# Cross-attention and a table-GELU feed-forward on one core: bias work, clears and one product moved, and TensorE products that nobody reads in the opening

## The chip, the core and the metric

The kernel runs on one core of a Trainium2 chip. The metric is the device time of one launch in microseconds (us), the median of several runs. The engines are named as the profile names them: PE is TensorE (matmuls and transposes), DVE is VectorE, ACT is ScalarE, POOL is GpSimd, SP is the engine that issues most DMAs.

## The reference, cut to what matters

Tokens: 64 sequences of 64, each of width 128, so 4,096 rows. The context has the same shape.

```
q  = layernorm(x) @ Wq.T + bq           # 16 heads of 8
kv = ctx @ Wkv.T + bkv                  # k and v interleaved in the last axis
q, k = rms_norm(q) * q_gamma, rms_norm(k) * k_gamma
x  = x + softmax(q k^T / sqrt(8)) v     # within each sequence of 64

h  = layernorm(x) @ w1 + b1             # 128 -> 512
h  = round(h * 256) / 256
h  = interp(h, 33 points of GELU on [-4, 4]), 0 below, identity above, rounded again
x  = x + round((h @ w2 + b2) * 256) / 256
```

## The kernel before

Each engine has its own instruction stream, written out by hand, and they meet only at semaphores. An engine runs its stream strictly in the order in which it is written. There is no scheduler.

**Setup.** The two projection weights are loaded and transposed on PE, and DVE copies them out of PSUM (L698 to L704). Biases are added by a matmul: a bias row is split into three float16 parts that sum to it (`bias_parts`, stages 0 to 4, L719 to L727) and multiplied by a matrix that picks the parts. This is done once for the attention (`B_Q` to `B_1`) and once for the feed-forward (`ffn_bias`), where `w1` and `b1` are also scaled by 256 (L790, L794). Four buffers `v_blk` hold v in blocks, zero elsewhere, with ones that give the softmax's denominator. They are cleared once, 0 and 1 by DVE (`clear_v`, L590), 2 and 3 by POOL (L382), and POOL writes the ones (L371, L387).

**Attention.** There are 16 steps of 2 tiles (256 tokens). `step(s)` on each engine does the stages of several neighbouring steps, as a software pipeline, and starts with `step(-3)`, `step(-2)` or `step(-1)`. For step s + 1 DVE's `step(s)` does `mean_square` (L617, needs ACT's square L435), `bias_v` (L654, needs PE's `project_v` L974), `normalise` (L624) and `highs` (L635, L637), for step s `copy_parts` (L644), for s - 1 `heads_out` (L664, L666), for s - 2 the feed-forward's layer norm (`ln2_statistics` L606, `norm_x2` L611), and for s + 3 `ln_statistics` (L600). POOL's `step(s)` does `norm_x` for s + 2 (L309 to L315), `lows` for s + 1 (L334), and smaller pieces. PE's `step(s)` does `transpose_parts(s)` (L992), `times_v(s - 1)` (L1022), `project_v(s + 1)`, `scores(s)` (L1006), `transpose_in(s + 2)` (L943, L948), `out_back(s - 1)` (L1032) and `project_qk(s + 2)` (L955, L935, L960, L964). `transpose_in(s)` waits for `bias_v(s - 1)`, and `project_qk(s)` for `normalise(s - 1)`, since they share PSUM banks.

**Feed-forward.** There are 8 groups of 4 tiles, each in two units of 1,024 columns. Per unit: hidden product (PE, L1128 and L1129), rounding (ACT, L513), split into segment and fraction (DVE, `f_segment` L829, `f_fraction` L835), two GELU look-ups (ACT, L521 and L530), difference and slope (DVE, `f_rise` L842, `f_slope` L850), the sum (POOL, `f_interpolate` L406, which waits for a `frac_ready` of the next group), rounding (DVE, `f_round` L856), down product (PE, L1144), and the residual (DVE, `f_out` L862). Between the two parts PE writes the first hidden product in two halves (`hidden_first(0)` and `(1)`, L1163), which DVE rounds (`round_first`, L818).

**Start of the attention.** DVE's stream goes `step(-2)`, then `scale_w1` and the first half of the feed-forward's bias work, then `step(-1)`, then the rest of it, then `step(0)`. POOL's stream goes `step(-2)`, ones for two buffers, `step(-1)`, clears and ones for the other two, `step(0)`. A check of a bound on the scores (`guarded`) stands between. It loads one value and branches, and its body isn't run with these inputs.

Of the kernel before, what the change touches and what calls it, by code (L numbers as in the profile page):

```python
# [40 lines left out]
P = 128  # L41
# [31 lines left out]
def xattn_ffn(nc, x_d, ctx_d, wq_d, bq_d, wkv_d, bkv_d, gq_d, gk_d, w1_d, b1_d, w2_d, b2_d, out_d):  # L73
# [11 lines left out]
    with ctx:  # L85
# [210 lines left out]
        def _(pool):  # L296
# [69 lines left out]
            pool.wait_ge(S["v_zeroed"], 2)  # L366
            for k in range(2):
                for half in range(2):

                    wait(pool, "blocks_set", 2 * k + half)  # L370
                    g.memset(v_blk[k][64 * half:64 * half + 64, :, :, half, DH:DH + 1].rearrange("p b q e -> p b (q e)"), 1.0).then_inc(S["blocks_set"], 1)  # L371
            pool.wait_ge(S["blocks_set"], 4)
# [8 lines left out]
            for k in range(2, 4):  # L381
                g.memset(v_blk[k][:, :, :, :, :].rearrange("p b q h e -> p (b q h e)"), 0.0).then_inc(S["v_zeroed"], 1)  # L382
            pool.wait_ge(S["v_zeroed"], 4)
            for k in range(2, 4):
                for half in range(2):
                    wait(pool, "blocks_set", 2 * k + half)
                    g.memset(v_blk[k][64 * half:64 * half + 64, :, :, half, DH:DH + 1].rearrange("p b q e -> p b (q e)"), 1.0).then_inc(S["blocks_set"], 1)  # L387
            pool.wait_ge(S["blocks_set"], 8)
# [192 lines left out]
        def _(dve):  # L581
# [146 lines left out]

            dve.wait_ge(S["small_loaded"], 16 * 4)
# [62 lines left out]
            ffn_bias = slice(B_1, B_END)  # L792
            scale_w1()
# [3 lines left out]
            step(-1, 3)  # L797
            for stage in range(2, 5):
                bias_parts(ffn_bias, stage, "ffn_ready")
            for s in range(0, LOOP_FROM):  # L800
                step(s, s % 4)
# [62 lines left out]
            def group(gr):  # L864
                f_rise(gr, 0)
                f_slope(gr, 0)
                if gr >= 1:
                    f_round(gr - 1, 1)
                if gr + 1 < GROUPS:
                    f_segment(gr + 1, 0)  # L870
                    f_fraction(gr + 1, 0)
                if gr == 1:
                    norm_x2(STEPS - 1)
# [23 lines left out]
            ln2_statistics(STEPS - 2)  # L897
            f_segment(0, 1)
            f_fraction(0, 1)
            norm_x2(STEPS - 2)  # L900
# [23 lines left out]
        def _(pe):  # L924
            t_ = nc.tensor
            pe.wait_ge(S["wqkv_loaded"], 16 * 2)
            pe.wait_ge(S["identity_ready"], 1)
# [3 lines left out]
            last.then_inc(S["w_transposed"], 1)  # L931

# [241 lines left out]
            scores(last_step, 0)  # L1174
            scores(last_step, 1)
# [3 lines left out]
            hidden_first(0)  # L1179
            out_back(last_step - 1)  # L1180
# [61 lines left out]
```

## Time and profile before

| | |
|---|---|
| median of 3 runs | 220.64 us (218.24 to 221.98) |
| the profiled execution | 219.01 us, of which the trace's span is 217.1 us |
| PE busy | 184.1 us (85%) |
| DVE busy | 189.3 us (87%) |
| ACT busy | 146.3 us (67%) |
| POOL busy | 117.9 us (54%) |
| mean granted TensorE clock | 0.959 |

In the trace the opening takes 0 to 32 us, the steady attention steps 32 to 118 us, the turn to the feed-forward 118 to 140 us and the feed-forward the rest. A row of a timeline gives the start, the duration of the group, engine, line, operation, operands, the count, and in brackets how long the engine was idle before it and what ended that.

### The profile page before, as it was taken

Reading aid. Unit: us, or ns where it says so; the run is one execution under the profiler, and the core shown is the slowest. Engines: PE = TensorE matmul, PEld = TensorE weight load, DVE = VectorE, ACT = ScalarE, POOL = GpSimd, SP = SyncE. Lnnn points to the kernel's source line nnn. Section 1 sums busy time; section 2 is a strip of 40 time slices with the busy share of each in tenths; the row PEclk is TensorE's granted clock in tenths of the full one; section 3 lists DMA queues with packets and bytes.
Section 4 is the critical chain, followed back from the end, with each engine's and each line's share of the span. In section 5 each row is a group of like instructions: output and inputs, shape, how many; then the busy total and the mean of one; then the engine's idle time right before and its main releaser. Section 6 shows DMA issues by size and latency. Waiting matters only on the chain.

```text
span 217.1 us, 8020 instructions
## 1 busy us (share of the span) xinstructions
PE 184.1 (85%) x3308; PEld 143.5 (66%) x3308; DVE 189.3 (87%) x348; ACT 146.3 (67%) x226; POOL 117.9 (54%) x166
## 2 busy tenths in 40 slices
PE   1172889999999999999999789959799999986693
PEld 0161768888888888888888645456566566654592
DVE  6628968799999999999999757999999999999992
ACT  2021367778977778987777778867487878878511
POOL 7330864687677687767675501465165444655430
PEclk9996699999999999999999999988999999999679
DMA  4270111011211011100000000000101011010103
GB/s 110 82 206 10 51 53 49 14 44 51 54 53 49 27 32 53 51 27 29 8 3 3 3 3 2 3 0 0 48 5 48 0 48 51 0 48 0 48 0 97
DMA packets 14835, 7.95 MB, mean 37 GB/s; under 512 B 1072, under 2 KB 14576, under 8 KB 14800
## 3 DMA queue, kind: packets, MB, share of 16 engines
q1 hardware_dynamic: 14272, 7.20, 11.6%
q8 instruction: 26, 0.43, 0.8%
q10 hardware_dynamic: 528, 0.25, 0.4%
q14 instruction: 9, 0.07, 0.1%
HBM read 5.35 MB, written 2.10 MB: 34 GB/s over the span
## 4 chain that ended last, share of the span: by engine, by line
PE 44%; DVE 23%; issue 13%; POOL 13%; DMA 2%; ACT 1%; SPq 1%; DVEq 0%; POOLq 0%; ACTq 0%
POOL y_raw L406 8%; PE bank_o L1022 8%; PE banks_p L992 7%; PE banks_p L964 5%; PE banks_s L1006 5%; DVE frac L835 4%; DVE banks_p L842 4%; PE banks_p L974 4%; PE bank_o L1032 4%; PE banks_p L960 3%; DMA bkv_rep<-in_L_xattn_bkv_dram 2%; DVE y_raw L850 2%; DVE act_q L856 2%; PE banks_p L943 2%; DVE seg L829 2%
## 5 line engine op out<-in xcount | busy, mean ns | idle before, releaser
L406 POOL TENSOR_TENSOR y_raw<-g_lo,y_raw 128x1024 f32<-128x1024 f32 x15 | 35.4, 2363 | 36.4 <-DVE frac L835 35.4
L1144 PEld LDWEIGHTS bank_o<-w,act_q 128*128 128x128 f32 x224 | 29.9, 211 | 6.6 <-DVE act_q L856 5.9
L460 ACT ACTIVATE probs<-banks_s 128x512 f32<-128x512 f32 x64 | 33.0, 610 | 1.2 <-PE banks_s L1006 1.1
L334 POOL TENSOR_TENSOR parts<-qk_hat,parts 128x512 f16<-128x512 f32 x16 | 18.6, 1160 | 26.6 <-DVE parts L635 26.6
L1144 PE MATMUL bank_o<-w,act_q 128*128 128x128 f32 x224 | 31.4, 299 | 1.5 <-DVE act_q L856 1.3
L1129 PE MATMUL banks_s<-x2T,w 128*128 128x512 f32 x60 | 31.2, 602 | 0.0
L521 ACT ACTIVATE g_lo<-seg,gelu_lo 128x1024 f32<-128x1024 f32 x16 | 18.4, 1150 | 9.1 <-DVE seg L829 9.1
L530 ACT ACTIVATE banks_p<-seg,gelu_hi 128x1024 f32<-128x1024 f32 x16 | 17.9, 1118 | 8.8 <-DVE y_raw L850 8.8
L992 PE MATMUL banks_p<-ident,parts 128*128 128x128 f16 x256 | 19.6, 219 | 1.8 <-POOL parts L334 1.6
L1022 PE MATMUL bank_o<-probs,v_blk 128*32 128x64 f32 x1024 | 20.7, 222 | 0.0
L611 DVE TENSOR_SCALAR xn_all<-x_all,stats,rstd 128x128 f32<-128x128 f32 x32 | 20.1, 667 | 0.0
L850 DVE SCALAR_TENSOR_TENSOR y_raw<-banks_p,frac 128x1024 f32<-128x1024 f32 x16 | 19.6, 1224 | 0.5
L842 DVE TENSOR_TENSOR banks_p<-banks_p,g_lo 128x1024 f32<-128x1024 f32 x16 | 19.6, 1224 | 0.4 <-ACT banks_p L530 0.4
L430 ACT ACTIVATE xcT<-banks_p 128x512 f32<-128x512 f32 x16 | 9.6, 597 | 13.7 <-PE banks_p L948 13.7
L1022 PEld LDWEIGHTS bank_o<-probs,v_blk 128*32 128x32 f32 x1024 | 15.7, 109 | 3.9 <-issue 0.9
L992 PEld LDWEIGHTS banks_p<-ident,parts 128*128 128x128 f16 x256 | 14.8, 97 | 4.8 <-issue 2.0
L455 ACT ACTIVATE outT<-bank_o 128x512 f32<-128x512 f32 x16 | 9.5, 597 | 12.3 <-PE bank_o L1022 12.3
L450 ACT ACTIVATE partsT<-banks_p 128x1024 f16<-128x1024 f16 x16 | 16.4, 1022 | 0.8 <-PE banks_p L992 0.8
L513 ACT ACTIVATE hz<-banks_s,round_c 128x1024 f32<-128x1024 f32 x15 | 16.4, 1096 | 0.0
L1129 PEld LDWEIGHTS banks_s<-x2T,w 128*128 128x128 f32 x60 | 11.7, 195 | 6.8 <-issue 5.7
L943 PE MATMUL banks_p<-ident,c_in 128*128 128x128 f32 x32 | 7.4, 316 | 9.6 <-DVE wqgT L749 4.9
L654 DVE TENSOR_TENSOR v_blk<-banks_p,bv_rep 64x256 f32<-64x256 f32 x32 | 13.5, 421 | 2.1 <-PE banks_p L974 0.7
(114 smaller groups left out, 427.4 us busy)
## 6 DMA issues: line engine op xcount, KB each, us to landing
x_all<-in_x_dram SPq DMA_DIRECT2D x16, 128.0 KB, 2.9
c_in<-in_ctx_dram SPq DMA_DIRECT2D x16, 128.0 KB, 2.4
out_dram<-x_all SPq DMA_DIRECT2D x7, 256.0 KB, 2.3
w<-in_L_ffn_w_dram SPq DMA_DIRECT2D x2, 256.0 KB, 3.2
out_dram<-x_all SPq DMA_DIRECT2D x2, 128.0 KB, 1.9
b_rows<-in_L_ffn_b_dram SPq DMA_DIRECT2D x1, 192.0 KB, 3.6
wkv_raw<-in_L_xattn_Wkv_dram ACTq DMA_DIRECT2D x1, 128.0 KB, 2.9
bkv_rep<-in_L_xattn_bkv_dram SPq DMA_DIRECT2D x1, 128.0 KB, 5.4
```

The lines of the kernel that those rows point to most:

```text
L334: g.tensor_tensor(low_slot, qk_hat[:].rearrange("p w t (h d) -> p w (t h) d", d=DH), high_slots[:, :, :, 0, :], ALU.subtract).then_inc(S[" ...
L406: g.tensor_tensor(y_raw[u][:], g_lo[n % 3][:], y_raw[u][:], ALU.add).then_inc(S[f"gelu{u}_done"], 1)
L460: a.activation(probs[i][:].rearrange("p t g n -> p (t g n)"), bank_s(i), ACT.Exp).then_inc(S["probs_ready"], 1)
L521: a.activation(g_lo[n % 3][:], seg0[u][:], ACT.Gelu, bias=gelu_lo[:], scale=1.0 / FIX).then_inc(S["glo_ready"], 1)
L530: a.activation(g_hi, seg0[u][:], ACT.Gelu, bias=gelu_hi[:], scale=1.0 / FIX).then_inc(S["ghi_ready"], 1)
L611: v.tensor_scalar(xn2_all[:, tok(s, t, 2)], x_all[:, tok(s, t, 2)], stats2[:, t, 1:2], rstd2[:, t:t + 1], ALU.subtract, ALU.mult).then_inc ...
L842: v.tensor_tensor(g_hi, g_hi, g_lo[n % 3][:], ALU.subtract).then_inc(S["rise_ready"], 1)
L850: v.scalar_tensor_tensor(y_raw[u][:], g_hi, 1.0 / SEG, frac[u][:], ALU.mult, ALU.mult).then_inc(S["slope_done"], 1)
L992: last = t_.transpose(bank_qkT[:, c0:c0 + P], rows[:, P * k:P * k + P], ident16[:])
L1022: last = t_.matmul(bank_o[ROWS * i:ROWS * i + ROWS, c0:c0 + 64], v_blk[par][:, 2 * t + b, 2 * i + gg, :, :].rearrange("p h e -> p (h e)"), ...
L1129: last = t_.matmul(out, w1[:, f0:f0 + P], x2T[gr % 2][:], start=False, stop=True)
L1144: last = t_.matmul(out, act_q[u][:, c, P * t:P * t + P], w2[:, CH // UNITS * u + c, :], start=False, stop=(u == UNITS - 1 and t == GT - 1 ...
```

## The change

- PE: at its start 6, and after the weights' transposes 10, matmuls of the 128x128 identity with 512 columns of it, float16, into `bank_o`, which nobody reads there (`keep_busy`).
- DVE: `clear_v(2)` is added behind the copies of the weights. `step(-1)` now stands ahead of `scale_w1` and the first half of the feed-forward's bias work, `step(0)` ahead of stages 2 and 3, `step(1)` ahead of stage 4.
- POOL: the clear of `v_blk` 3 and all the ones go between `step(-2)` and the bound check. `v_blk` 2 is no longer POOL's.
- PE at the turn: `hidden_first(0)` and its waits go ahead of the last step's `scores`.
- DVE in the feed-forward: `norm_x2(STEPS - 2)` goes ahead of `f_segment(0, 1)`, and in group 1 `norm_x2(STEPS - 1)` ahead of `f_segment(2, 0)` and `f_fraction(2, 0)`.

```diff
@@ gpsimd
             step(-2)
-            pool.wait_ge(S["v_zeroed"], 2)
-            for k in range(2):
+            g.memset(v_blk[3][:, :, :, :, :].rearrange("p b q h e -> p (b q h e)"), 0.0).then_inc(S["v_zeroed"], 1)
+            pool.wait_ge(S["v_zeroed"], 4)
+            for k in range(4):
                 for half in range(2):
                     wait(pool, "blocks_set", 2 * k + half)
...
-            pool.wait_ge(S["blocks_set"], 4)
+            pool.wait_ge(S["blocks_set"], 8)
...
             step(-1)
-            for k in range(2, 4):
-                g.memset(v_blk[k][:, :, :, :, :].rearrange("p b q h e -> p (b q h e)"), 0.0).then_inc(S["v_zeroed"], 1)
-            pool.wait_ge(S["v_zeroed"], 4)
-            for k in range(2, 4):
-                for half in range(2):
...
@@ vector
+            clear_v(2)
             dve.wait_ge(S["small_loaded"], 16 * 4)
...
+            step(-1, 3)
             scale_w1()
             setup(v.tensor_scalar(b_rows[:, B_1:B_2], b_rows[:, B_1:B_2], FIX, None, ALU.mult))
             bias_parts(ffn_bias, 0, "ffn_ready")
             bias_parts(ffn_bias, 1, "ffn_ready")
-            step(-1, 3)
-            for stage in range(2, 5):
-                bias_parts(ffn_bias, stage, "ffn_ready")
-            for s in range(0, LOOP_FROM):
+            step(0, 0)
+            bias_parts(ffn_bias, 2, "ffn_ready")
+            bias_parts(ffn_bias, 3, "ffn_ready")
+            step(1, 1)
+            bias_parts(ffn_bias, 4, "ffn_ready")
+            for s in range(2, LOOP_FROM):
                 step(s, s % 4)
...
+                if gr == 1:
+                    norm_x2(STEPS - 1)
                 if gr + 1 < GROUPS:
                     f_segment(gr + 1, 0)
                     f_fraction(gr + 1, 0)
-                if gr == 1:
-                    norm_x2(STEPS - 1)
...
             ln2_statistics(STEPS - 2)
+            norm_x2(STEPS - 2)
             f_segment(0, 1)
             f_fraction(0, 1)
-            norm_x2(STEPS - 2)
@@ tensor
+            def keep_busy(n):
+                for _ in range(n):
+                    t_.matmul(bank_o[:], ident16[:], ident16[:].unsqueeze(1).to_broadcast([P, 4, P]), start=True, stop=True)
+
+            pe.wait_ge(S["identity_ready"], 1)
+            pe.wait_ge(S["consts_ready"], 1)
+            keep_busy(6)
             pe.wait_ge(S["wqkv_loaded"], 16 * 2)
-            pe.wait_ge(S["identity_ready"], 1)
...
             last.then_inc(S["w_transposed"], 1)
+            keep_busy(10)
...
-            scores(last_step, 0)
-            scores(last_step, 1)
             pe.wait_ge(S["ffn_ready"], 2)
             pe.wait_ge(S["qk_normed"], STEPS)
             pe.wait_ge(S["x2_t_copied"], 2)
             hidden_first(0)
+            scores(last_step, 0)
+            scores(last_step, 1)
             out_back(last_step - 1)
```

DVE around `step(-1)`, before. The first four rows are the scaling and stages 0 and 1, the six from `ms` to `stats` are `step(-1)`, and the two behind them are stages 2 and 3 (`b_rest` holds what is left of a bias after its float16 part):

```order
L790 TENSOR_SCALAR w1<-w1 128x512
L794 TENSOR_SCALAR b_rows<-b_rows 96x512
L719 CAST b_parts<-b_rows 96x640
L721 TENSOR_TENSOR b_rest<-b_rows,b_parts 64x640
L617 TENSOR_REDUCE ms<-qk_sq 128x64
L654 TENSOR_TENSOR v_blk0<-banks_p,bv_rep 64x32x8 x2
L624 TENSOR_TENSOR qk_hat<-banks_p,rms_inv 128x512
L635 CAST parts<-qk_hat 128x2x32x16
L637 COPY parts<-minus_max 128x32
L600 BN_STATS stats<-x_all 128x6
L723 CAST b_parts<-b_rest 64x640
L725 TENSOR_TENSOR b_rest<-b_rest,b_parts 32x640
```

The same place on DVE in the changed kernel, up to the first row of `step(0)`:

```order
L610 TENSOR_REDUCE ms<-qk_sq 128x64
L647 TENSOR_TENSOR v_blk0<-banks_p,bv_rep 64x32x8 x2
L617 TENSOR_TENSOR qk_hat<-banks_p,rms_inv 128x512
L628 CAST parts<-qk_hat 128x2x32x16
L630 COPY parts<-minus_max 128x32
L593 BN_STATS stats<-x_all 128x6
L784 TENSOR_SCALAR w1<-w1 128x512
L789 TENSOR_SCALAR b_rows<-b_rows 96x512
L712 CAST b_parts<-b_rows 96x640
L714 TENSOR_TENSOR b_rest<-b_rows,b_parts 64x640
L610 TENSOR_REDUCE ms<-qk_sq 128x64
L647 TENSOR_TENSOR v_blk1<-banks_p,bv_rep 64x32x8 x2
```

The four rows of scaling and splitting now stand behind `step(-1)` and directly ahead of `step(0)`, and the three stages that stood there are gone from this place.

POOL between `lows(0)` (`parts`) and `norm_x(2)` (`var_eps`, `xn`), before:

```order
L334 TENSOR_TENSOR parts<-qk_hat,parts 128x2x32x8
L382 MEMSET v_blk2 128x1024
L382 MEMSET v_blk3 128x1024
L387 MEMSET v_blk2 64x32 x2
L387 MEMSET v_blk3 64x32 x2
L309 TENSOR_SCALAR var_eps<-stats 128x2
```

POOL in the changed kernel behind the first layer norm, where the clear of buffer 3 and the ones stand now:

```order
L315 TENSOR_TENSOR xn<-xn,rstd 128x256
L366 MEMSET v_blk3 128x1024
L372 MEMSET v_blk0 64x32 x2
L372 MEMSET v_blk1 64x32 x2
```

Two more pairs of rows with ones follow it there, for buffers 2 and 3, and between `lows(0)` and `norm_x(2)` nothing is left.

## Rows read from the trace of the kernel before

**Rows 1.** The page: busy time and share of the span.

```profile
PE 184.1 (85%) x3308; PEld 143.5 (66%) x3308; DVE 189.3 (87%) x348; ACT 146.3 (67%) x226; POOL 117.9 (54%) x166
```

**Rows 2.** Windows: stretch, length, busy time by engine, granted clock (PEclk), DMA.

```profile
11.60:15.00 3.40, 3.36 (x14) 2.83 (x14) 0.76 (x4) 0.00 (x1) 2.04 (x4) 1.00 0.86 247
15.00:18.30 3.30, 0.69 (x16) 0.58 (x16) 1.23 (x3) 0.60 (x1) 0.00 (x0) 1.00 0.37 100
20.70:25.10 4.40, 4.06 (x18) 3.40 (x19) 4.29 (x5) 0.60 (x1) 2.83 (x3) 0.50 0.22 63
...
31.90:118.00 86.10, 85.81 (x2438) 73.04 (x2442) 80.09 (x169) 69.91 (x134) 61.01 (x103) 1.00 0.12 35
...
144.70:148.00 3.30, 3.30 (x13) 2.50 (x12) 3.13 (x4) 2.94 (x4) 2.36 (x1) 0.50 0.00 0
```

**Rows 3.** Timeline of the opening, all engines, 2.8 to 12 us.

```profile
2.86 1.89 POOL L361 MEMSET parts<- 128x2144 f16 x1
...
4.03 0.91 DVE L590 MEMSET v_blk<- 128x1024 f32 x1 [0.16 <-issue]
...
4.09 0.48 PE L928 MATMUL banks_p<-ident,wq_raw 128*128 128x128 f32 x1 [4.09 <-DMA wkv_raw<-in_L_xattn_Wkv_dram]
...
8.17 0.17 DVE L732 SCALAR_TENSOR_TENSOR gqk<-gq_rep,gk_rep 128x8 f32<-128x8 f32 x1 [2.00 <-DMA bkv_rep<-in_L_xattn_bkv_dram]
...
9.85 0.69 PE L943 MATMUL banks_p<-ident,c_in 128*128 128x128 f32 x2 [4.86 <-DVE wqgT L749]
...
11.64 0.58 PE L955 MATMUL banks_p<-b_parts,pick 128*128 128x512 f16 x1 [0.67 <-DVE b_parts L727]
```

**Rows 4.** Timeline, PE: one product of the same shape, step 0 and step 2.

```profile
12.23 1.06 PE L960 MATMUL banks_p<-wqT,xcT 128*128 128x128 f32 x4
...
30.14 0.61 PE L960 MATMUL banks_p<-wqT,xcT 128*128 128x128 f32 x4
```

**Rows 5.** Timeline, DVE and ACT, 15 to 40 us.

```profile
15.03 0.60 ACT L435 ACTIVATE qk_sq<-banks_p 128x512 f32<-128x512 f32 x1 [3.43 <-PE banks_p L964]
...
17.04 0.43 DVE L790 TENSOR_SCALAR w<-w 128x512 f32<-128x512 f32 x1 [4.61 <-DMA b_rows<-in_L_ffn_b_dram]
...
17.83 0.49 DVE L719 CAST b_parts<-b_rows 96x640 f16<-96x640 f32 x1
...
19.21 0.69 DVE L617 TENSOR_REDUCE ms<-qk_sq 128x64 f32<-128x512 f32 x1
...
22.53 3.02 DVE L723 CAST b_parts<-b_rest 64x640 f16<-64x640 f32 x1
...
26.85 0.67 DVE L617 TENSOR_REDUCE ms<-qk_sq 128x64 f32<-128x512 f32 x1
...
32.41 0.69 DVE L617 TENSOR_REDUCE ms<-qk_sq 128x64 f32<-128x512 f32 x1 [1.51 <-ACT qk_sq L435]
...
39.06 0.69 DVE L617 TENSOR_REDUCE ms<-qk_sq 128x64 f32<-128x512 f32 x1 [1.04 <-ACT qk_sq L435]
```

**Rows 6.** Timeline, POOL and PE, 23 to 32 us.

```profile
23.37 1.85 POOL L382 MEMSET v_blk<- 128x1024 f32 x2
...
30.55 1.16 POOL L334 TENSOR_TENSOR parts<-qk_hat,parts 128x512 f16<-128x512 f32 x1 [1.75 <-DVE parts L635]
...
31.97 0.61 PE L992 MATMUL banks_p<-ident,parts 128*128 128x128 f16 x8 [0.33 <-POOL parts L334]
```

**Rows 7.** Timeline, DVE: the second layer norm's scaling at three places.

```profile
114.81 1.28 DVE L611 TENSOR_SCALAR xn_all<-x_all,stats,rstd 128x128 f32<-128x128 f32 x2
...
134.51 0.60 DVE L611 TENSOR_SCALAR xn_all<-x_all,stats,rstd 128x128 f32<-128x128 f32 x2
...
148.97 2.67 DVE L611 TENSOR_SCALAR xn_all<-x_all,stats,rstd 128x128 f32<-128x128 f32 x2
```

**Rows 8.** Timeline, ACT at the turn to the feed-forward.

```profile
128.51 1.28 ACT L564 ACT_TABLE_LOAD   x1
...
131.11 1.15 ACT L521 ACTIVATE g_lo<-seg,gelu_lo 128x1024 f32<-128x1024 f32 x1 [1.32 <-DVE seg L829]
```

More of the change, by code:

```diff
@@ L380, in _ @@
             step(-1)
-            for k in range(2, 4):
-                g.memset(v_blk[k][:, :, :, :, :].rearrange("p b q h e -> p (b q h e)"), 0.0).then_inc(S["v_zeroed"], 1)
-            pool.wait_ge(S["v_zeroed"], 4)
-            for k in range(2, 4):
-                for half in range(2):
-                    wait(pool, "blocks_set", 2 * k + half)
-                    g.memset(v_blk[k][64 * half:64 * half + 64, :, :, half, DH:DH + 1].rearrange("p b q e -> p b (q e)"), 1.0).then_inc(S["blocks_set"], 1)
-            pool.wait_ge(S["blocks_set"], 8)
             for s in range(0, LOOP_FROM):
```

## The prediction

> **What bounds the kernel now.** I read the page first: PE 85%, DVE 87% [rows 1], so neither engine has much room, but these are means over stages with different limits. The windows by stage come next. From 31.9 to 118 us PE is busy 85.81 of 86.10 us [rows 2]: there only PE counts, the change touches nothing in it, and whatever the opening gains arrives whole at the start of the feed-forward. The opening is another case. PE has 0.69 us of work between 15.0 and 18.3 us and afterwards a granted clock of 0.50 to 25.1 us [rows 2]. The timeline says who is late: ACT's square of step 0 is there at 15.03 + 0.60 = 15.63, but DVE takes it up at 19.21 only, because its stream has the feed-forward's scaling first, and that waited 4.61 us for a load, to 17.04 [rows 5]. The same happens again with the next square: DVE is in a cast of 3.02 us from 22.53 on, and `mean_square(1)` starts at 26.85 with no idle time ahead of it [rows 5]. It leads to `lows(1)` at 30.55 and to PE's transposes at 31.97, where PE's unbroken work begins [rows 6]. So the end is set by DVE's order up to 32 us, by PE to 118, and by the DVE and POOL chain behind it.
>
> **The moved bias work, `step(-1)` first.** If PE is as slow as now, `mean_square(0)` starts at 15.65 instead of 19.21. Of the old block from 19.21 to the cast at 22.53, 3.32 us long [rows 5], `bias_v(0)` now waits a little for PE's 0.69 us of v products, so I take 3.5 us: `step(-1)` ends at 19.2. The four instructions of scaling and stages 0 and 1 took 19.21 - 17.04 = 2.17 us [rows 5] with POOL idle, and the load that they need has landed by 17.04. They end at 21.4, with nothing in their way. The three stages behind are gone from here. `mean_square(1)` would start then, if its input is there.
>
> That input passes through PE: transposes, 12 projection products, ACT. In step 0 four of these products took 1.06 us, in step 2 0.61 [rows 4], so 12 cost about 3 x 0.45 = 1.3 us more at the low clock. Starting from `bias_v(0)` as in the old trace I get the square of step 1 ready at about 22.2 if PE is slow, 20.8 if it isn't.
>
> **POOL beside it.** The four instructions now meet POOL's `lows(0)` and `norm_x(2)`, where before they had it idle. The trace bounds what that costs. From below: a pair of L611 took 0.60 us alone [rows 7]. From the middle: the same pair beside two POOL additions took 1.28, so 0.34 us more for each [rows 7]. From above: the cast of 3.02 us beside POOL's clears, where a larger cast took 0.49 [rows 5, 6], 2.5 us more. The additions are what stands beside the block now, so I take 0.34, 4 x 0.34 = 1.4 us, and the ends are 0 and 10.
>
> The Trainium skill (SBUF — State Buffer, "SBUF: two separate sides") speaks against this move: by it DVE, in its fast modes and with two SBUF inputs, and GpSimd hold their shared port pair by an exclusive lock for a whole instruction, and the other is blocked. The pair of 1.28 us agrees with waiting as such; whether each instruction waits its full turn is a rival below.
>
> **Reading nobody's products.** The 6 products cover PE's wait up to the transposes at 4.09 [rows 3]. 512 columns at 1.2 GHz are 0.43 us each, so from about 2.0 they last to 4.6 and put the transposes, and DVE's copies, half a microsecond back. DVE waits 2.00 us for a load behind these copies, to 8.17 [rows 3]. Into the same gap goes `clear_v(2)`, 0.91 us like its sisters [rows 3]: 0.5 + 0.9 = 1.4, under 2.00, so both cost nothing. If that cover were gone, they would cost 1.4. DVE's clear ran 0.91 us beside POOL's of 1.89 us [rows 3], so the two clears don't hold each other up. The 10 further products end at 9.8 if all are slow and at about 8 if the clock rises, ahead of PE's next work at 9.85 [rows 3], and that has 0.67 us of slack at 11.64 [rows 3]. POOL's larger batch of clears and ones ends some 1.7 us later than now and meets nothing before 12 us.
>
> What they buy is the clock in step 0. The page's clock column isn't to be read there: it says 1.00 from 11.6 to 15.0 [rows 2], while the products last 1.06 us instead of 0.61 [rows 4]. If PE is fast by 11.64, the 12 products and the two bias products end 1.5 us sooner and all of the above moves by 1.5. PE was at work without a pause from 20.7 to 25.1 before its clock rose, and 3.3 us with 0.69 us of work cost it the clock [rows 2]. The new products give a stretch of work of the first sort from 2.0 to 8. Between 8 and 11.6 lies a nearly idle stretch of the second sort, though. I take it that the clock holds, as the likelier, at 0.6.
>
> With it: `mean_square(0)` at 14.15, `step(-1)` to 17.7, the four to 19.9 and with POOL 21.3, the square of step 1 ready by 19.4. So `mean_square(1)` starts at 21.3 instead of 26.85: **-5.5 us**. With a slow PE all is 1.5 later: -4.0.
>
> **Stages 2 to 4.** After `step(0)` DVE had 1.51 us idle [rows 5]. Stages 2 and 3 need 0.4 + 0.85 (the cast by 0.49, the subtraction by what is left of the block to 19.21 [rows 5]) = 1.3 us, 2.0 with two waits for POOL. What goes over delays `mean_square(2)` by 0.5, of which `copy_parts(1)` passes on perhaps 0.3: **+0.3**. Stage 4 fits 0.5 us into 1.04 us [rows 5]. POOL's clears (1.85 us [rows 6]) and their ones leave the stretch for good, which pays for xn(2) and is inside the -5.5.
>
> **The turn.** PE does the same work in another order, 1.1 us of product ahead of the scores. `out_back`, which the residual needs, ends when it did. ACT's exponentials and its table load, 128.51 to 129.79, come 1.1 us later, 130.9, and its next look-up began at 131.11 after waiting 1.32 us for DVE [rows 8]. So it just fits: **0**, bounds -0.6 and +0.6. `norm_x2(14)` moves into DVE's wait for a rounded unit: 0.
>
> **`norm_x2(15)`.** In group 1 the pair takes 2.67 us, from 148.97 on, in POOL's shadow, against 0.60 alone [rows 7]. POOL starts that sum on `frac_ready`. With the pair ahead of segment and fraction POOL is idle and can't start, and the pair takes 0.60; `f_rise` follows 2.07 us sooner. ACT's rounding of the first output waits for PE's down product, which doesn't move, and eats about 0.3. **-1.75**, bounds -2.07 and -1.0.
>
> **The sum.** -5.5 + 0.3 + 0 - 1.75 = -6.95, from the profiled execution's 219.01: 212.1 us. That execution lies 1.6 us below the median of the runs shown. I add about half of that, 0.9, since a median of three over 218.2 to 222.0 isn't firm: **213.0 us**.
>
> **Rivals.**
> - *The clock does not hold.* The gap from 8 to 11.6, or the thin PE work of 15 to 24 us, brings it down again. Then -4.0 + 0.3 - 1.75 = -5.45, 213.6 on the same execution, 214.5 as a median. For: 0.69 us in 3.3 was enough for it [rows 2]. Chance 0.25. If it is low still when PE's unbroken work begins, another 1 to 2 us go, 216.
> - *POOL costs DVE nothing.* The four instructions slip between POOL's. Then `mean_square(1)` is at 19.9 and the sum is -8.65, 211.3. For: a cast and `b_rest` may be too short to be caught. Chance 0.12.
> - *Each of the four waits out a whole POOL instruction.* `lows` takes 1.16 us [rows 6], and the first meets the second half of it; the others meet the layer norm's shorter ones, some 0.6 us each going by half of that. That is 2.4 us instead of 1.4, so 1 us more and 214.0. The skill's lock rule, taken literally, gives this. Chance 0.1.
> - *The later gains are given back.* PE's down products and the next hidden ones hold the chain in group 1, or the late exponentials cost their 1.1 us. Then -5.2 alone, 214.7. For: PE is busy at a clock of 0.50 to 148 us [rows 2]. Chance 0.1.
> - *Slower.* If each moved DVE instruction is shut out as the cast of 3.02 us was, for 2.5 us [rows 5], the block costs 10 us more, stages 2 and 3 5, stage 4 2: 17 - 6.95 - 1.4 (already counted) - 0.7 (slack) = +8, 228. It turns slower from about 1.3 us for each of the seven. Against: that cast stood beside two clears with no gap between them, and the clears are gone. Chance 0.03.
> - *No change that counts:* the steady part starts no sooner, because a load or xn(1) is what is late. Against: PE waits for DVE at each of these places. Chance 0.03.
>
> The forecast's own case has the rest, 0.37. The range takes in the clock, both prices of POOL and the lost later gains, and leaves the two last out: 209.8 to 216.5. What this kernel's runs can tell from no change is about 2%, 4.4 us: below 216.2 it is faster. From the cases: faster 0.89, same 0.08, slower 0.03.
>
> **What would show it.** Right: the L617 instances at 14.2 and 21.3 us, PE's unbroken work from about 26.5 instead of 31.97, the first four-product group of L960 at 0.61 us, the L611 pair of group 1 at 0.60 us, exponentials ending close to the first look-up. Wrong: 1.06 us for the first L960 (clock), a scaling or cast of over 1 us behind `step(-1)` (POOL), an idle DVE ahead of the second L617 (PE or a load is late), a wait ahead of the last group-1 instructions (given back).

## The result, and the profile after

| | median, us | runs | profiled run | its span | its granted clock |
|---|---|---|---|---|---|
| before | 219.44 | 4 (217.44 to 221.98) | 219.01 | 217.1 | 0.959 |
| after | 211.52 | 4 (209.99 to 211.96) | 211.96 | 210.1 | 0.973 |

The changed kernel is faster: ratio 0.966 [0.955, 0.977]. The forecast was 213.0 with 209.8 to 216.5 around it; on the profiled execution it was 212.1, and that took 211.96. The page's row of busy times answers to [rows 1]:

```profile
PE 186.5 (89%) x3324; PEld 142.8 (68%) x3324; DVE 188.0 (89%) x349; ACT 146.3 (70%) x226; POOL 118.6 (56%) x165
```

Busy times are nearly what they were. PE's is 2.4 us longer: the products that nobody reads add 6.3 (2.72 and 3.55 below), and the rest of its work took 3.9 less, in the opening, where the clock was higher. The 7 us came out of waits. The timeline of the changed kernel's opening, all engines (start, busy us, engine, line, operation; in brackets the idle time before and what ended it), answers to [rows 3, 4]:

```profile
2.06 2.72 PE L927 MATMUL bank_o<-ident 128*128 128x512 f16 x6 [2.06 <-POOL ident L353]
...
5.21 3.55 PE L927 MATMUL bank_o<-ident 128*128 128x512 f16 x10
6.76 0.91 DVE L583 MEMSET v_blk<- 128x1024 f32 x1 [0.16 <-issue]
7.06 0.95 POOL L366 MEMSET v_blk<- 128x1024 f32 x1
8.03 0.17 DVE L726 SCALAR_TENSOR_TENSOR gqk<-gq_rep,gk_rep 128x8 f32<-128x8 f32 x1 [0.36 <-DMA bkv_rep<-in_L_xattn_bkv_dram]
...
11.83 0.61 PE L966 MATMUL banks_p<-wqT,xcT 128*128 128x128 f32 x4
```

DVE's row at 8.03 still waits for its load, 0.36 us instead of 2.00, so the added clear and the later copies had their cover. The four products of step 0 take 0.61 us instead of 1.06: PE runs at 2.4 GHz there, not at 1.2; the trace's record of the clock has it at 1.00 from 7.69 us on. Next the timeline of DVE and POOL around the moved block, which answers to [rows 5, 6]:

```profile
13.99 0.69 DVE L610 TENSOR_REDUCE ms<-qk_sq 128x64 f32<-128x512 f32 x1 [1.70 <-ACT qk_sq L428]
...
17.31 1.16 POOL L334 TENSOR_TENSOR parts<-qk_hat,parts 128x512 f16<-128x512 f32 x1 [2.73 <-DVE parts L628]
17.57 1.18 DVE L784 TENSOR_SCALAR w<-w 128x512 f32<-128x512 f32 x1
18.67 0.41 DVE L789 TENSOR_SCALAR b_rows<-b_rows 96x512 f32<-96x512 f32 x1
18.76 0.79 POOL L310 TENSOR_TENSOR xn<-x_all,stats 128x256 f32<-128x256 f32 x1
19.11 0.79 DVE L712 CAST b_parts<-b_rows 96x640 f16<-96x640 f32 x1
19.52 0.93 POOL L312 TENSOR_TENSOR rstd<-var_eps,minus_half 128x2 f32<-128x2 f32 x1
19.93 0.82 DVE L714 TENSOR_TENSOR b_rest<-b_rows,b_parts 64x640 f32<-64x640 f32 x1
20.78 0.69 DVE L610 TENSOR_REDUCE ms<-qk_sq 128x64 f32<-128x512 f32 x1
...
24.77 1.24 DVE L716 CAST b_parts<-b_rest 64x640 f16<-64x640 f32 x1
25.92 0.61 PE L998 MATMUL banks_p<-ident,parts 128*128 128x128 f16 x8 [0.33 <-POOL parts L334]
26.05 1.27 DVE L718 TENSOR_TENSOR b_rest<-b_rest,b_parts 32x640 f32<-32x640 f32 x1
27.35 0.69 DVE L610 TENSOR_REDUCE ms<-qk_sq 128x64 f32<-128x512 f32 x1
```

The reader is to see three things. `mean_square(0)` starts at 13.99 instead of 19.21. The scaling of 0.43 us takes 1.18 beside POOL's `lows`: it waits until `lows` is over at 18.47 and ends 0.3 us later. And `mean_square(1)` starts at 20.78 with no wait ahead of it, as before at 26.85, so DVE is still what bounds this stretch; PE's unbroken work begins at 25.92 instead of 31.97. The same view of DVE in the feed-forward answers to [rows 7]:

```profile
142.93 0.60 DVE L604 TENSOR_SCALAR xn_all<-x_all,stats,rstd 128x128 f32<-128x128 f32 x2
```

The pair of group 1 takes 0.60 us instead of 2.67. How the gain of 7 grew and shrank on its way, by the start of the same instruction in both traces:

| instruction | before | after | difference |
|---|---|---|---|
| `mean_square(0)` | 19.21 | 13.99 | -5.22 |
| `mean_square(1)` | 26.85 | 20.78 | -6.07 |
| PE's transposes, step 1 | 31.97 | 25.92 | -6.05 |
| `lows(15)` | 120.56 | 115.50 | -5.06 |
| `f_rise(0, 0)`, first of the feed-forward | 135.02 | 130.18 | -4.84 |
| `f_rise(1, 1)` | 151.56 | 144.65 | -6.91 |
| last `f_rise` | 206.24 | 199.34 | -6.90 |
| span | 217.1 | 210.1 | -7.0 |

6.05 us are won in the opening, 1.0 is lost in the steady part, 0.2 lost again at the turn, 2.07 won in group 1, and nothing is given back behind it. Of the loss of 1.0 the forecast had 0.3, for stages 2 to 4.

### The profile page after: what moved, and what is told of

The parts are those of the page before. It is cut to its first block, busy times and chain, and to the rows that moved or that the text cites. A ratio compares the mean times of both kernels' runs of the same rounds, so it can differ in the third digit from the quotient of the medians.

```text
span 210.1 us, 8050 instructions
## 1 busy us (share of the span) xinstructions
PE 186.5 (89%) x3324; PEld 142.8 (68%) x3324; DVE 188.0 (89%) x349; ACT 146.3 (70%) x226; POOL 118.6 (56%) x165
## 4 chain that ended last, share of the span: by engine, by line
PE 47%; DVE 23%; POOL 13%; issue 11%; DMA 2%; SPq 1%; ACT 0%; DVEq 0%; POOLq 0%
PE bank_o L1028 8%; PE banks_p L998 8%; POOL y_raw L399 8%; PE banks_p L970 6%; PE banks_s L1012 5%; DVE frac L832 5%; DVE banks_p L839 4%; PE banks_p L980 4%; PE bank_o L1038 4%; DVE y_raw L847 3%; PE banks_p L966 3%; DMA bkv_rep<-in_L_xattn_bkv_dram 2%; DVE act_q L853 2%; PE banks_p L949 2%; DVE seg L826 2%
## 5 line engine op out<-in xcount | busy, mean ns | idle before, releaser
L1150 PEld LDWEIGHTS bank_o<-w,act_q 128*128 128x128 f32 x224 | 29.2, 208 | 6.7 <-DVE act_q L853 6.5
L1150 PE MATMUL bank_o<-w,act_q 128*128 128x128 f32 x224 | 30.7, 295 | 1.2 <-DVE act_q L853 1.0
L1135 PE MATMUL banks_s<-x2T,w 128*128 128x512 f32 x60 | 30.6, 592 | 0.0
L998 PE MATMUL banks_p<-ident,parts 128*128 128x128 f16 x256 | 20.3, 224 | 1.7 <-POOL parts L334 1.4
L604 DVE TENSOR_SCALAR xn_all<-x_all,stats,rstd 128x128 f32<-128x128 f32 x32 | 17.7, 595 | 1.1 <-POOL rstd L328 1.1
L998 PEld LDWEIGHTS banks_p<-ident,parts 128*128 128x128 f16 x256 | 15.4, 100 | 4.6 <-issue 2.3
L1012 PE MATMUL banks_s<-partsT 32*64 32x64 f16 x1024 | 13.7, 196 | 1.3 <-issue 0.8
```

Of the source, the lines that this page charges most:

```text
L998: last = t_.transpose(bank_qkT[:, c0:c0 + P], rows[:, P * k:P * k + P], ident16[:])
L1012: last = t_.matmul(bank_s(i)[64 * half:64 * half + 64, c0:c0 + 64], partsT[t][rg, 1, k, cols], partsT[t][rg, 0, k, cols], start=True, stop ...
L1135: last = t_.matmul(out, w1[:, f0:f0 + P], x2T[gr % 2][:], start=False, stop=True)
L1150: last = t_.matmul(out, act_q[u][:, c, P * t:P * t + P], w2[:, CH // UNITS * u + c, :], start=False, stop=(u == UNITS - 1 and t == GT - 1 ...
```

## Experiments

Four sets were run. The kernel before had a median of 219.09, 218.46, 219.71 and 218.50 us in them, and each ratio is against its own set's.

### Set 1: each part alone, and the change without its unread products

**no_busy**, the change without them:

```diff
-            keep_busy(6)
...
-            keep_busy(10)
```

> The changed kernel without the 16 products that nobody reads. Theory (they buy the clock of step 0 and nothing else): the first four L960-type products take 1.06 us again instead of 0.61, mean_square(0) starts 1.5 us later than in the changed kernel (at about 15.6 instead of 13.99), mean_square(1) at 22.3 instead of 20.78, PE's unbroken work at 27.4 instead of 25.92, and the time is 213.0. Rival (DVE's order alone makes the gain, PE's clock is hidden): mean_square(1) stays at 20.8 and the time at 211.5.

Measured: 211.96 us (210.78 to 213.38), 0.971 [0.966, 0.976]. Its timeline:

```profile
11.66 1.06 PE L964 MATMUL banks_p<-wqT,xcT 128*128 128x128 f32 x4
...
13.23 0.39 PE L968 MATMUL banks_p<-wqgT,xcT 128*128 128x128 f32 x2
...
14.51 0.69 DVE L610 TENSOR_REDUCE ms<-qk_sq 128x64 f32<-128x512 f32 x1 [2.64 <-ACT qk_sq L428]
...
18.13 1.06 PE L964 MATMUL banks_p<-wqT,xcT 128*128 128x128 f32 x4
...
21.29 0.69 DVE L610 TENSOR_REDUCE ms<-qk_sq 128x64 f32<-128x512 f32 x1
```

The first products are slow (1.06), yet the later ones are not (0.39 for a pair): the clock rose in the middle of the step, by the trace's record at 13.07 us. From the first product to `mean_square(0)` it is 2.85 us, against 2.16 with the unread products: in this execution they would have bought 0.7 us, not 1.5. In step 1 the clock is low again (1.06 at 18.13) and costs nothing: `mean_square(1)` follows 6.78 us after `mean_square(0)`, against 6.79, because DVE has its block of bias work to do anyway. The median, 0.4 us above the change's, can't tell 0.7 us from nothing; the trace does.

**only_busy**, the kernel before with just those 16 products added:

```diff
+            keep_busy(6)
...
+            keep_busy(10)
```

> The kernel before, with the 16 products added and nothing else. Theory: PE ends step 0's products 1.5 us sooner, but DVE stands at the load and the scaling until 19.2, so mean_square(0) does not move and the time stays at that of before, 219.4. Rival (a faster clock helps by itself): 1 to 2 us less, about 218.

Measured: 219.29 us, 1.000 [0.996, 1.005]. Its timeline:

```profile
11.19 0.61 PE L969 MATMUL banks_p<-wqT,xcT 128*128 128x128 f32 x4
...
16.34 0.43 DVE L790 TENSOR_SCALAR w<-w 128x512 f32<-128x512 f32 x1 [4.68 <-DMA b_rows<-in_L_ffn_b_dram]
```

PE has its clock in step 0, and DVE waits 4.68 us for the load all the same, with the square long there; `mean_square(0)` starts at 18.51. A faster engine in front of one that waits for something else is worth nothing.

**only_swap**, the kernel before with `norm_x2(STEPS - 1)` moved:

```diff
                 if gr == 1:
+                    norm_x2(STEPS - 1)
                 if gr + 1 < GROUPS:
                     f_segment(gr + 1, 0)
                     f_fraction(gr + 1, 0)
-                if gr == 1:
-                    norm_x2(STEPS - 1)
```

> The kernel before, with norm_x2(15) ahead of f_segment(2, 0) and f_fraction(2, 0) and nothing else. Theory: the pair of scalings takes 0.60 us instead of 2.67, f_rise(1, 1) starts 2.07 us sooner, and all of it reaches the end: 217.4. Rival (later waits for PE's down product give it back): f_rise is sooner, but the last group is not, 219.4.

Measured: 216.27 us, 0.990 [0.986, 0.994], so 2.2 us by the ratio (the medians differ by 2.8). Its timeline of DVE:

```profile
146.39 0.60 DVE L611 TENSOR_SCALAR xn_all<-x_all,stats,rstd 128x128 f32<-128x128 f32 x2
148.10 1.22 DVE L842 TENSOR_TENSOR banks_p<-banks_p,g_lo 128x1024 f32<-128x1024 f32 x1
```

0.60 us again, and 4.95 us from one `f_rise` to the next where before it was 7.02: the step is worth its 2.07 us whole.

**only_bias**, the kernel before with DVE's new order of bias work, while POOL's clears stay:

```diff
+            step(-1, 3)
             scale_w1()
...
-            step(-1, 3)
-            for stage in range(2, 5):
+            step(0, 0)
+            for stage in range(2, 4):
                 bias_parts(ffn_bias, stage, "ffn_ready")
+            step(1, 1)
+            bias_parts(ffn_bias, 4, "ffn_ready")
```

> The kernel before, with the bias work in DVE's new order and nothing else: POOL keeps its clears, no products that nobody reads. Theory: mean_square(0) starts at 15.6, the four moved instructions meet POOL's lows and its clears, so they take 3 to 5 us instead of 2.17; mean_square(1) at 23 to 24.5 instead of 26.85, and the time is 216 to 217. Rival (POOL costs DVE nothing): mean_square(1) at 22.3, 214.9. Rival (shut out like the cast of 3.02 us): mean_square(1) at 26 or later, no gain, 219.

Measured: 217.58 us, 0.992 [0.988, 0.996]. Its timeline:

```profile
18.51 2.96 DVE L790 TENSOR_SCALAR w<-w 128x512 f32<-128x512 f32 x1
19.34 1.85 POOL L382 MEMSET v_blk<- 128x1024 f32 x2
...
23.24 0.69 DVE L617 TENSOR_REDUCE ms<-qk_sq 128x64 f32<-128x512 f32 x1
```

The scaling of 0.43 us takes 2.96: it is shut out for the rest of `lows(0)` (18.25 to 19.4) and both clears, to 21.2. `mean_square(1)` comes 3.6 us ahead of the old kernel's, and so does PE's unbroken work, at 28.38; 0.7 of that is no part of the edit, since the first product came at 11.50 instead of 12.23. Yet the time gained 1.8 only. In its steady part single steps of this execution are longer by 0.17, 0.44, 0.68, 0.22 and 0.76 us, 2.3 in all, where the old kernel's have 0.4; that was the first sign of the loss found above. At the turn the clock was low (14.76 us from `lows(15)` to `f_rise(0, 0)`, 14.46 in the old kernel's profile).

### Set 2: one part taken back at a time

**clears_back**, the change with POOL's clears of buffers 2 and 3 back behind `step(-1)`:

```diff
@@ gpsimd
-            g.memset(v_blk[3]...)
...
             step(-1)
+            for k in range(2, 4):
+                g.memset(v_blk[k]...)
@@ vector
-            clear_v(2)
```

> The changed kernel with POOL clearing v_blk 2 and 3 and writing their ones behind lows(0) again, and without DVE's third clear. Theory (POOL's clears shut DVE's moved instructions out): from mean_square(0) to mean_square(1) 8.3 us, as in the run with the bias order alone, instead of 6.8; PE's unbroken work starts 1.5 us later, the time is 213.0. Rival (where POOL clears is without effect, the layer norm behind them does the same): 6.8 us, 211.5.

Measured: 212.72 us, 0.970 [0.964, 0.976]. Its timeline:

```profile
11.93 1.06 PE L972 MATMUL banks_p<-wqT,xcT 128*128 128x128 f32 x4
...
19.08 2.95 DVE L790 TENSOR_SCALAR w<-w 128x512 f32<-128x512 f32 x1
19.91 1.85 POOL L382 MEMSET v_blk<- 128x1024 f32 x2
...
23.81 0.69 DVE L617 TENSOR_REDUCE ms<-qk_sq 128x64 f32<-128x512 f32 x1
```

The shut-out is back, to a hundredth the 2.96 of only_bias, and `mean_square(1)` follows 8.45 us after `mean_square(0)` instead of 6.79. So moving the clears is worth 1.7 us in the trace; the medians differ by 1.2 and their intervals overlap. A second thing is in these rows: this kernel has all 16 unread products, and its first real ones still take 1.06 us. The record of its clock has the rise at 7.87 us, behind the unread products, and a fall at 11.28, behind a stretch in which PE had 1.60 us of work in 3.30. Its window of step 0 (stretch, length, busy times of PE, PEld, DVE, ACT, POOL, granted clock, DMA):

```profile
11.30:14.60 3.30, 3.26 (x14) 2.82 (x14) 0.77 (x4) 0.00 (x0) 2.04 (x4) 0.50 0.83 250
```

In the change's own profile PE had as little work there (1.73 us in 3.50), and the clock stayed up.

**hidden_back**, the change with `hidden_first(0)` behind the scores again:

```diff
+            scores(last_step, 0)
+            scores(last_step, 1)
...
             hidden_first(0)
-            scores(last_step, 0)
-            scores(last_step, 1)
```

> The changed kernel with the first hidden product behind the last scores again. Theory: PE does the same work, out_back ends when it did, the exponentials come 1 us sooner and nobody needs them sooner; 211.5 within 0.4. Rival (DVE gains by rounding the first half while it waits): the change is worth 0.6, so this is 212.1. Rival (the late exponentials cost): this is 210.8.

Measured: 211.67 us, 0.969 [0.963, 0.975], which tells nothing at this size. The trace: from `lows(15)` to `f_rise(0, 0)` 14.09 us, against 13.32 to 13.37 in five executions with the new order (no_busy, busy_first_only, act_scales, and act_three and after_again of set 3). The other three with it took longer: 13.77 in clears_back, whose scores have a pause of their own, and 14.68 and 14.85 in the change's profile and in act_scales_busy of set 4, where the clock fell. PE's rows at its turn, and those of the second execution of the unchanged kernel before (**before_again**, set 3):

```profile
119.44 0.25 PE L1012 MATMUL banks_s<-partsT 32*64 32x64 f16 x4
120.26 0.76 PE L1012 MATMUL banks_s<-partsT 32*64 32x64 f16 x60 [0.57 <-issue]
```

```profile
125.39 0.34 PE L1006 MATMUL banks_s<-partsT 32*64 32x64 f16 x20
126.21 0.61 PE L1006 MATMUL banks_s<-partsT 32*64 32x64 f16 x44 [0.48 <-issue]
```

PE stops for 0.57 and 0.48 us in the middle of 64 small products, at the 5th in one and the 21st in the other, waiting for nothing that the profile shows. All four executions with the old order and a high clock have such a pause, of 0.48 to 0.81 us. With `hidden_first(0)` ahead the products run through, in 0.81 us, in seven of eight executions; clears_back pauses for 0.19. That step, priced at 0, is worth about 0.8 us.

**busy_first_only**, the change with the first six unread products only:

```diff
-            keep_busy(10)
```

> The changed kernel with the first 6 products that nobody reads and without the 10 behind the transposes. Theory: PE is idle from 5.3 to 9.7 us and the first four projection products run at the low clock again, 1.06 us instead of 0.61; then all is like the run without any such product, mean_square(0) 2.8 us or more after the first of these products instead of 2.16, 212.0 or a little more. Rival (the first 6 are enough): 0.61 us and 211.5.

Measured: 212.25 us, 0.969 [0.963, 0.975]. Its timeline of PE:

```profile
9.73 0.69 PE L948 MATMUL banks_p<-ident,c_in 128*128 128x128 f32 x2 [4.31 <-DVE wqgT L743]
...
12.06 1.06 PE L965 MATMUL banks_p<-wqT,xcT 128*128 128x128 f32 x4
```

With 4.31 us of nothing ahead of 9.73 the first six leave no trace: 2.86 us from the first product to `mean_square(0)`, as without any.

**act_scales**, the change with the two scalings of the feed-forward's weights and bias on ACT:

```diff
@@ scalar
             step(-1)
+            act.wait_ge(S["ffw_loaded"], 16 * 4)
+            a.activation(b_rows[:, B_1:B_2], b_rows[:, B_1:B_2], ACT.Copy, scale=FIX).then_inc(S["b_scaled"], 1)
+            a.activation(w1[:], w1[:], ACT.Copy, scale=FIX).then_inc(S["ffn_ready"], 1)
@@ vector
-            scale_w1()
-            setup(v.tensor_scalar(b_rows[:, B_1:B_2], b_rows[:, B_1:B_2], FIX, None, ALU.mult))
+            dve.wait_ge(S["b_scaled"], 1)
```

> The changed kernel with the two scalings by 256 (w1 and the bias row) on ACT, between its step(-1) and step(0), instead of on DVE. Theory (mean_square(1) waits only for DVE's four instructions): DVE's block has two instructions, from mean_square(0) to mean_square(1) 5.7 us instead of 6.8, PE's unbroken work 1.1 us sooner, 210.4. Rival (ACT's two instructions delay its square of step 1, or the first cast is shut out until lows ends so that nothing is won): 6.6 us or more, 211.5.

Measured: 210.45 us (208.90 to 212.23), 0.964 [0.959, 0.969]. Its timeline:

```profile
16.81 0.62 ACT L489 ACTIVATE b_rows<-b_rows 96x512 f32<-96x512 f32 x1
17.15 1.16 POOL L334 TENSOR_TENSOR parts<-qk_hat,parts 128x512 f16<-128x512 f32 x1 [2.87 <-DVE parts L633]
17.33 0.62 ACT L490 ACTIVATE w<-w 128x512 f32<-128x512 f32 x1
17.46 1.20 DVE L717 CAST b_parts<-b_rows 96x640 f16<-96x640 f32 x1
18.68 0.61 POOL L310 TENSOR_TENSOR xn<-x_all,stats 128x256 f32<-128x256 f32 x1
18.70 1.27 DVE L719 TENSOR_TENSOR b_rest<-b_rows,b_parts 64x640 f32<-64x640 f32 x1
...
20.00 0.69 DVE L615 TENSOR_REDUCE ms<-qk_sq 128x64 f32<-128x512 f32 x1
```

Two instructions with 1.6 us of DVE time in the change are gone, but `mean_square(1)` follows in 6.29 us, only 0.5 sooner: now the cast waits for `lows` (1.20, where it took 0.49 with POOL idle) and the subtraction for POOL's subtraction (1.27, where beside the power on 2 columns it took 0.82). ACT's scaling beside `lows` took 0.62, both times.

### Set 3: further on ACT, and both kernels once more

**act_three**, act_scales with the first cast on ACT as well:

```diff
+            a.activation(b_parts[0:BR, B_1:B_END], b_rows[:, B_1:B_END], ACT.Copy).then_inc(S["b_scaled"], 1)
...
@@ vector
-            dve.wait_ge(S["b_scaled"], 1)
-            bias_parts(ffn_bias, 0, "ffn_ready")
+            dve.wait_ge(S["b_scaled"], 2)
```

> The run with the two scalings on ACT, with the first cast of the bias on ACT as well, so that DVE has only the subtraction of stage 1 between step(-1) and step(0). Theory: that subtraction has two SBUF inputs and waits for POOL's lows to end, so from mean_square(0) to mean_square(1) 5.8 us instead of 6.3, and another 0.4 us less in all. Rival (ACT has no room: its square of step 1 comes later and DVE waits for it): 6.3 us or more, and no gain.

Measured: 212.89 us (210.28 to 213.38), 0.968 [0.964, 0.973]. Its timeline:

```profile
17.66 1.06 PE L972 MATMUL banks_p<-wqT,xcT 128*128 128x128 f32 x4
...
20.80 0.69 DVE L618 TENSOR_REDUCE ms<-qk_sq 128x64 f32<-128x512 f32 x1 [0.82 <-ACT qk_sq L428]
```

DVE is idle for 0.82 us now, waiting for the square that PE's slow products made late. In this stretch PE at the low clock stands right behind DVE: its slack was what no_busy had used.

**after_again** and **before_again**, both kernels unchanged, one execution each:

> The changed kernel unchanged, profiled a second time. Theory (the pauses in PE's score products, 0.61, 0.16 and 0.46 us in the first profile, and the low clock at the turn are chance, not the change): the first 26 us repeat within 0.5 us, the extra time of the steady steps lies in other steps, 0 to 1.5 us in all, and the turn takes 13.3 us from lows(15) to f_rise(0, 0) instead of 14.68 if the clock holds there. Rival (they belong to the changed program): the same steps are long again by the same amounts, and the clock falls at 116 to 120 us again.

> The kernel before unchanged, profiled a second time. Theory: opening as in the first profile within 1 us (PE's unbroken work at 31 to 32 us), other steps long, 0 to 1.5 us in all, and at the turn the last scores again have a pause of 0.4 us or more, or run at the low clock. Rival: identical steps long by identical amounts, 0.27 and 0.16.

Measured: 211.52 and 218.92 us. The opening repeats: `mean_square` at 14.00 and 20.79 (13.99 and 20.78 in the first). What doesn't repeat is the clock at the start of the unbroken part. In after_again the transposes took 1.06 us, and by the record the clock was low from 24.53 to 27.94 us. Its window of 26 to 29.5 us holds the end of that, with PE busy throughout:

```profile
26.00:29.50 3.50, 3.50 (x80) 2.98 (x82) 2.57 (x5) 2.11 (x4) 2.48 (x4) 0.72 0.01 1
```

The first step is 1.08 us too long. Ahead of the fall PE had 1.78 us of work in the 3.20 from 21.3 to 24.5 us, and it had the same in the change's first profile, where the clock stayed up. The small losses of the steady part are there in both kernels, and they repeat in part: the third whole step is 0.61 us too long in the first profile of the change and 0.67 in the second, while the 0.46 of the twelfth is gone; in the kernel before the seventh is long both times (0.16 and 0.28), and the 0.74 of the tenth is new.

### Set 4: the clock kept up in step 1

**act_scales_busy**, act_scales with four more unread products ahead of the transposes of steps 1 and 2:

```diff
@@ tensor, in step
+                if isinstance(s, int) and s in (-1, 0):
+                    keep_busy(4)
                 transpose_in(...)
```

> The run with the two scalings on ACT (210.45 us), with 4 more products that nobody reads in each of the two places where PE waits for DVE in steps -1 and 0 (ahead of transpose_in(1) and transpose_in(2)). Theory: they fill about 0.9 us of each wait of 1.0 us and delay nothing; the clock no longer falls between 13 and 30 us, which some executions show (first projection products of step 1 at 1.06 us, transposes of step 1 at 1.06 us); PE's unbroken work at 25.1 as in the run without them, and the median 0.3 lower, near 210. Rival (the products make PE late for the transposes that DVE's copies free): ms(1) or PE's unbroken work 0.3 us or more later, 210.7.

Measured: 211.98 us (209.73 to 212.90), 0.965 [0.959, 0.970]. Its timeline of PE:

```profile
17.28 0.61 PE L970 MATMUL banks_p<-wqT,xcT 128*128 128x128 f32 x4
```

The clock held in steps 0 to 2, as it had in the profile of act_scales without them, and PE's unbroken work began at 25.33 (25.13 in act_scales, whose opening started 0.25 earlier), but no time came of it: DVE bounds the stretch, and the profiled execution lost 1.6 us in the steady part. The lowest median stays that of act_scales, whose interval overlaps the change's; whether it is a better kernel isn't settled.

## Why the prediction was right, and where its terms were off

The mechanism, the place of each gain and the total came out. Of its marks `mean_square(0)` was forecast at 14.15 and came at 13.99, `mean_square(1)` at 21.3 and 20.78, PE's unbroken work at 26.5 and 25.92, the pair of group 1 at 0.60 and 0.60. Term by term:

- **The block behind `step(-1)`: right, and the reason too.** The load no longer holds DVE up, and DVE's own work sets `mean_square(1)`. -6.07 against -5.5. 0.4 of the difference is no part of the change: the first product came at 12.23 in the old kernel's profile and at 11.83 in this one, and over the fourteen profiled executions of this study it lies anywhere between 11.19 and 12.23.
- **POOL beside it: 1.04 us against 1.4.** The block takes 3.21 us (17.57 to 20.78) instead of 2.17. The price isn't 0.34 for each: the first pays 0.75, waiting for the end of `lows`, the second nothing, the cast 0.30, the subtraction nothing beside the power on 2 columns and 0.45 beside POOL's subtraction (act_scales). So which POOL instruction it meets decides, and where it waits, it waits for that one's end. The scaling and the cast agree with the rule of the Trainium skill (SBUF — State Buffer, "SBUF: two separate sides"), by which DVE and GpSimd lock the port pair that they share for a whole instruction. The subtraction beside the power doesn't: it has two inputs in SBUF and started 0.41 us into the power, yet took the 0.82 of a free one, and there the measurement decides. The rival built on the rule, 2.4 us, failed since only two of the four waited. POOL pays too: its subtraction took 0.79 us instead of 0.61 and the power 0.93 instead of 0.70.
- **The slower rival's mechanism is real, its condition wasn't met.** 2.5 us of shut-out for a moved instruction is what only_bias and clears_back show beside `lows` and two clears without a gap. The change took the clears away in the same edit. Without that it would have lost 1.7 us of its gain, not turned slower, since only the first of the seven is hit.
- **The clock: it held, but bought 0.7 or 1.3 us, not 1.5.** The working set a PE slow for all of the step against a fast one, whose way from the first product to `mean_square(0)` is 2.16 us. How slow PE is without the products differs from execution to execution. In no_busy and busy_first_only the clock rose halfway through the step by itself (2.85 and 2.86 us). In the other four executions without the ten products (both of the kernel before, only_swap and only_bias) it rose at the step's end (the forecast's 15.65 less 12.23 is 3.42; only_bias took 3.44), so against these the products are worth 1.3. Six executions are too few to say which is the rule; the medians of no_busy and busy_first_only lie 0.4 and 0.7 us above the change's. Nor is the clock sure: of eight executions with both groups seven had 0.61 and one 1.06. And in step 1 a low clock has DVE's block for cover. The rival "the clock does not hold" was priced at 214.5; no_busy, where it was low in the first half of the step, took 211.96. The forecast took for a model a stretch "without a pause from 20.7 to 25.1", which has 0.34 us of idle PE in it [rows 2].
- **Stages 2 to 4: 0.17 us against 0.3.** The cast and the subtraction took 1.24 and 1.27, waiting for POOL twice, and `mean_square(2)` came with no idle time. PE passed 0.17 of it on: the first whole step is 6.57 instead of 6.40 us in every undisturbed execution with the new order.
- **The turn: about -0.8 us against 0, beyond the bound of -0.6.** ACT's table load and look-up did just fit (the look-up at 126.45 waits 0.15 for DVE). `norm_x2(14)`, also priced at 0, gave some 0.2: before, its pair stands between the fraction and `f_rise(0, 0)` for 0.51 us, and now it runs in DVE's wait but makes the segment 0.3 late. What was missed is the pause inside the scores, 0.81 us in the profile before. It didn't show in the changed kernel's own profile, because there the clock fell. The windows (as above), with the last two rows at the turn:

```profile
25.90:113.00 87.10, 86.09 (x2443) 73.20 (x2446) 81.89 (x172) 69.72 (x134) 62.18 (x104) 1.00 0.12 34
...
115.80:116.90 1.10, 0.00 (x0) 0.02 (x1) 1.09 (x3) 1.10 (x3) 1.10 (x2) 1.00 0.00 0
116.90:120.00 3.10, 3.09 (x47) 2.60 (x48) 0.95 (x2) 1.85 (x3) 1.33 (x3) 0.50 0.02 5
```

PE had nothing to do for 1.10 us and then worked 3.1 us at 0.50 of full speed. Its turn took 14.68 us; with the clock up it is 13.3, as hidden_back's section lists. The old order shows 14.1 with a pause of 0.5 to 0.6.

- **`norm_x2(15)`: -2.07 us against -1.75.** ACT's rounding of the output did not eat 0.3, and the bound named for it was the true value.
- **Not foreseen: 0.8 us lost in the steady part.** The first of the windows has 1.0 us of PE idle in 87.1 us, the old kernel's had 0.3 in 86.1 [rows 2]. A step is 6.40 us, and the rest comes in single steps, up to 0.76 us too long, with pauses of up to 0.62 us inside the scores' small products. They come in executions of both kernels, partly in the same steps: beyond the 0.17, the old kernel lost 0.4 and 1.2 us, the change 1.2 and 1.0 (after_again, without its clock). So the sentence that the opening's gain arrives whole left out a loss that differs by 0.8 us between executions of one kernel. Over all profiled executions that loss is 0.7 on average for the four with the old order of bias work and 1.2 for the ten with the new one, which is too few to say whether the change adds to it.
- **The 0.9 us added for the median: not found.** The medians of the kernel before in the four sets, 218.46 to 219.71, lie around the 219.01 of its profiled execution. Without the 0.9 the forecast is 212.1, against 211.52.

So 6.95 forecast and 7.0 found is partly luck. Between the two profiles the block gave 0.55 more than its term, stages 2 to 4 0.13 and `norm_x2` 0.32, 1.0 us in all; the steady part took 0.8 of it, and the turn, with the low clock outweighing the missing pause, 0.2.

**What makes PE pause** no run settles, but the traces point at the loading of its instructions. The profile puts the pauses down to "issue". The page of the changed kernel lists a DMA queue that carries instructions (27 loads, 0.44 MB):

```profile
q8 instruction: 27, 0.44, 0.9%
```

Its records lie 3.3 us or more apart (4.8 on average) between `lows(1)` and the end of the turn. The fourteen traces have 36 pauses of 0.12 to 0.81 us there that are put down to "issue" and lie inside the scores' products, and every one of them ends 2.2 to 3.0 us after a load on q8 started. At the turn of after_again the load starts 2.8 us after `lows(15)`, as in before_again and hidden_back, and by the time that these two pause, PE is busy with the wide products of `hidden_first(0)` instead. So a run of small products that needs what is still being loaded would be what pauses, and wide products ahead would cover the wait. This is argued from times that coincide: no run changed the number or the order of the instructions in the steady part to test it.

## What to carry to other kernels

Look for the engine whose program order holds ready work behind a load, and move the load's consumer behind that work; but then count who it stands beside. Beside a long POOL instruction a short DVE scaling or cast waited until that one ended, and beside several without a gap until the last of them, so here a gap on POOL was worth more (1.7 us, clears_back) than two DVE instructions fewer (0.5, act_scales). Unread products that hold PE's clock pay only where PE's result is what the next engine waits for: 0.7 to 1.3 us here, and nothing where DVE was late anyway.

## What was not expected of the hardware

- **Pauses of PE in runs of small products**: up to 0.81 us, in rows of 64-column float16 matmuls, at places that differ in part between executions of one program, and each 2.2 to 3.0 us behind the start of a load of instructions.
- **The clock falls where PE isn't long idle, and not every time**: after 1.10 us at the turn (116.9 to 120 at 0.50) in the profiled execution of the change, and not in after_again with the same program and the same 1.1 us of idle PE; there it was low from 24.53 to 27.94 us instead. The second costs 0.9 us and the first 1.4.
- **Two clears don't hold each other up**: DVE's of 0.91 us at 6.76 ran beside POOL's of 0.95 at 7.06. DVE's other two in that trace take 0.91 too, and two of POOL's without a gap take 1.85 in the kernel before. A DVE scaling is shut out by such clears.
- **The clock column says 1.00 ahead of the first entry of its record**, whatever the products take: 1.06 us at 12.23 in the profile before [rows 2, 4]. That first entry is the clock's rise, at 14.89 us in the profile before, 13.07 in no_busy and 7.69 in the change. Ahead of it the length of one known product is the thing to read.
